# Preparing the bias table of a window-attention kernel: index columns in key-major order, compares ahead of statistics, small transfers of their own

## The reference

```
L0: window attention, windows of 8x8 = 64 tokens, 12 heads of 8 channels, biases on qkv and proj;
    attn = softmax(q k^T / sqrt(8) + rpb_table[rel_index])      rpb_table 225 x 12, rel_index 64 x 64
L1: shifted-window attention, 12 heads of 32 channels; dots + pos_emb[REL] + shift masks
L2: depthwise 3x3 and pointwise 1x1 convolution with ternary weights
L3: spiking attention with batch norms (integer counts 0..4)
```

## Time and profile before

| | |
|---|---|
| device time, 3 runs | 416.7, 419.48, 419.61 us; median 419.48 us |
| the profiled execution's own time | 419.33 us |
| its span, first to last instruction | 416.8 us |
| PE busy | 379.1 us (91%) |
| DVE, ACT, POOL busy | 314.7, 244.1, 200.3 us |
| share of the chain that ended last | PE 59%, DVE 21%, issue 11%, POOL 5%, ACT 2% |

### The profile page before, as it was taken

How to read it: one execution, slowest core, us unless ns; L and a number is a source line. 1 busy time by engine, 2 the same in 40 slices (tenths; PEclk the granted TensorE clock), 3 DMA queues, 4 the chain that set the end, 5 groups by cost and what they waited for, 6 DMA issues and landing times.

```text
span 416.8 us, 13469 instructions
## 1 busy us (share of the span) xinstructions
PE 379.1 (91%) x4953; PEld 275.6 (66%) x4953; DVE 314.7 (75%) x718; ACT 244.1 (59%) x571; POOL 200.3 (48%) x331
## 2 busy tenths in 40 slices
PE   4699999999999999999999999999998999958773
PEld 1588788888878777678777777877776433324441
DVE  3757878777788677978877777778879499856883
ACT  5235566666656555656565566665567355458871
POOL 6564657575767445343444344444444343433331
PEclk9999999999999999999999999999999999988996
DMA  8400000000000000000000000000000000000112
GB/s 187 97 4 4 3 2 0 0 0 0 2 2 3 2 2 2 2 2 2 3 2 0 0 0 0 0 2 0 2 4 2 0 1 0 2 0 19 40 39 57
DMA packets 8343, 5.06 MB, mean 12 GB/s; under 512 B 4874, under 2 KB 8074, under 8 KB 8306
## 3 DMA queue, kind: packets, MB, share of 16 engines
q1 hardware_dynamic: 7456, 4.43, 4.5%
q10 hardware_dynamic: 850, 0.12, 0.2%
HBM read 2.98 MB, written 1.57 MB: 11 GB/s over the span
## 4 chain that ended last, share of the span: by engine, by line
PE 59%; DVE 21%; issue 11%; POOL 5%; ACT 2%; POOLq 0%; DVEq 0%; ACTq 0%
PE bank L860 11%; PE bank L889 10%; PE bank L826 10%; PE bank L869 9%; PE bank L836 6%; DVE conv L1368 6%; PE bank L918 3%; PE bank L933 3%; DVE row_max L1065 3%; POOL y_out L1567 2%; DVE v L1024 2%; DVE stats L681 2%; PE bank L549 2%; PE bank L935 1%; PE bank L1476 1%
## 5 line engine op out<-in xcount | busy, mean ns | idle before, releaser
L1103 POOL TENSOR_TENSOR probs<-probs,row_max 128x384 f32<-128x384 f32 x128 | 105.3, 829 | 118.6 <-DVE row_max L1065 117.7
L967 ACT ACTIVATE probsT<-bank 128x384 f32<-128x384 f32 x128 | 61.1, 492 | 76.2 <-PE bank L869 76.2
L1061 DVE TENSOR_TENSOR probs<-bank,bias 128x384 f32<-128x384 f32 x128 | 65.3, 552 | 52.6 <-PE bank L860 52.3
L1065 DVE TENSOR_REDUCE row_max<-probs 128x6 f32<-128x384 f32 x128 | 68.3, 545 | 1.0
L869 PE MATMUL bank<-cst,probs 128*128 128x128 f32 x384 | 62.9, 281 | 0.0
L889 PE MATMUL bank<-v,probsT 128*64 128x18 f32 (+1 forms) x1536 | 57.7, 219 | 3.5 <-DVE headsN L1090 3.2
L889 PEld LDWEIGHTS bank<-v,probsT 128*64 128x64 f32 x1536 | 50.2, 137 | 15.0 <-issue 13.1
L860 PE MATMUL bank<-k,q 64*64 64x128 f32 x1536 | 58.0, 282 | 1.9 <-ACT k L1012 1.9
L860 PEld LDWEIGHTS bank<-k,q 64*64 64x64 f32 x1536 | 42.3, 135 | 21.8 <-issue 20.8
L1012 ACT ACTIVATE k<-bank,cst 128x256 f32<-128x256 f32 x128 | 54.0, 483 | 0.0
L869 PEld LDWEIGHTS bank<-cst,probs 128*128 128x128 f32 x384 | 44.7, 141 | 11.0 <-issue 5.0
(11 more groups left out here) (142 smaller groups left out, 549.2 us busy)
## 6 DMA issues: line engine op xcount, KB each, us to landing
x<-in_x SPq DMA_DIRECT2D x4, 384.0 KB, 7.3
out_dram<-y_out SPq DMA_DIRECT2D x8, 192.0 KB, 2.1
w<-in_L_conv_w_qkv SPq DMA_DIRECT2D x1, 432.0 KB, 4.9
cst<-in_consts SPq DMA_DIRECT2D x1, 304.0 KB, 5.8
p<-in_L_conv_w_out SPq DMA_DIRECT2D x1, 144.0 KB, 4.6
pos<-in_L_conv_pos_emb SPq DMA_DIRECT2D x8, 2.0 KB
cst<-in_consts SPq DMA_DIRECT2D x1, 117.0 KB, 3.5
w_raw<-in_L_conv_qkv_w ACTq DMA_DIRECT2D x1, 108.0 KB, 5.4
```

What stands on the lines that cost most here:

```text
L967: nc.scalar.activation(probsT[w][:, :], ps_probsT[w % 2][:, 0:NP * 128], ACT.Exp).then_inc(L.s.probsT_sb, 1)
L1061: nc.vector.tensor_tensor(out, scores, b, ALU.add).then_inc(L.s.biased, 1)
L1065: nc.vector.tensor_reduce(row_max[w][:, :], probs[w][:, :, :], AX.X, ALU.max).then_inc(L.s.maxed, 1)
L1103: nc.gpsimd.tensor_tensor(probs[w][:, :, :], probs[w][:, :, :], by_row(row_max[w]), ALU.subtract).then_inc(L.s.shifted, 1)
```

## The change

The diff does seven things. (1) The index copies write `rel_all` with columns in the order (key within a half, key half, query), so that in `onehot` the 128 columns of one key k (both halves, 64 queries each) are adjacent; one matmul with 128 stationary columns serves both halves, and there are 64 in place of 128. The writes of a copy thereby go 128 columns from element to element; a compare takes 64 runs of 16 columns in place of 1024 adjacent ones. (2) All four compares come ahead of the first statistics; the statistics of the third and fourth piece of x come after the bias, and the fourth after the first scores. (3) The identity (8 x 8) and the row numbers (128 x 2) that the spreading and the compares need are transfers of their own, issued by ACT; the bias table and L0's weights are issued by SP, the table behind `cst`, the weights behind the second piece of x. (4) The whole bias comes before the group-norm matmul, v of sample 0 before its scores, and `act_bias` before the evacuation of q. (5) POOL zeroes only `w0T` and `xn` before the table; after it come the rest for L0 and what L1 needs first (`v1`, `w1`), and only then the group norm. ACT's first exponential waits for `w0T` alone. (6) `pe_pos` becomes the extra job of sample 0. (7) The statistics of the second half of the batch are the job of sample 3 in place of sample 1, so samples 2 and 3 are written out and the loop starts at 4.

```diff
         def sp_loads(sp):
             sp.dma_start(cst[:, 0:N_FIRST], a["consts"][:, 0:N_FIRST]).then_inc(const_in, 16)
+            for dst, src in table_loads():
+                sp.dma_start(dst, src).then_inc(table_in, 16)
             n = B // N_X
             for i in range(N_X):
+                if i == N_X // 2:
+                    for dst, src in w0_loads():
+                        sp.dma_start(dst, src).then_inc(w0_in, 16)
                 sp.dma_start(x[:, i * n * T:(i + 1) * n * T].rearrange("c (b t) -> c b t", t=T),
...
+        def small_loads():
+            lo = CONSTS["ident"][0]
+            yield small_ident[:, :], a["consts"][0:REL_ROWS, lo:lo + REL_ROWS]
+            yield rel_of_row[:, :], a["consts"][0:REL_LO, CONSTS["rows"][0]:CONSTS["rows"][1]]
...
         @block.scalar
         def _(act):
-            for dst, src in table_loads():
-                act.dma_start(dst, src).then_inc(table_in, 16)
-            for dst, src in w0_loads():
-                act.dma_start(dst, src).then_inc(w0_in, 16)
+            for dst, src in small_loads():
+                act.dma_start(dst, src).then_inc(small_in, 16)
...
+        zero_first = [w0T[:, :], *(t[C:, :] for t in xn)]
+        zero_next = [p0T[C:, :], *(t[C:, :] for t in heads0), *(t[:, :, :, :] for t in v0)]
+        zero_wide = [*(t[:, :, :, :] for t in v1), w1[C:, :]]
+        zero_late = [w3_parts[C:, :, :], *(t[C:, :] for t in spike_in), spike_a[C:, :], *(t[:, :, :, :] for t in pad)]
...
                 step(nc.gpsimd.tensor_copy(table_parts[0:n_, t, 2, :], table_rest[0:n_, 1, t, :]))
+            for i, t in enumerate(zero_next):
+                nc.gpsimd.memset(t, 0.0).then_inc(zeroed, 1)
+                pool.wait_ge(zeroed, ZEROED_FIRST + i + 1)
+            pool_ones(v0, HD0, zeroed)
+            pool.wait_ge(zeroed, ZEROED)
+            for i, t in enumerate(zero_wide):
+                nc.gpsimd.memset(t, 0.0).then_inc(zeroed_late, 1)
+                pool.wait_ge(zeroed_late, i + 1)
+            pool_ones(v1, HD1, zeroed_late)
+            pool.wait_ge(zeroed_late, ZEROED_WIDE)
             pool.wait_ge(const_in, 16)
             pool_group_norm(pool, 0, 0)
...
+        def by_key(cols):
+
+            return cols.rearrange("r (g q) -> r g q", q=WT)
...
+            dve.wait_ge(small_in, SMALL_IN)
+            step(nc.vector.tensor_copy(small_ident_b[:, :], small_ident[:, :]))
             done["rel_rows"] = count[0]
...
-                cols = slice(2 * i * REL_COLS, 2 * (i + 1) * REL_COLS)
+                of = slice(2 * i * WIN, 2 * (i + 1) * WIN)
                 dve.wait_ge(rel_copied, 2 * i + 2)
                 for t in range(2):
-                    step(nc.vector.tensor_scalar(onehot[:, t, cols], rel_all[:, cols], cst[0:REL_LO, lo + t:lo + t + 1], None,
-                                                 ALU.is_equal))
...
+                    step(nc.vector.tensor_scalar(by_key(onehot[:, t, :])[:, :, of], by_key(rel_all)[:, :, of], rel_of_row[:, t:t + 1],
+                                                 None, ALU.is_equal))
+
+            for i in range(4):
+                compare(i)
+            done["onehot"] = count[0]
+            first_stats(dve, 0)
+            first_stats(dve, 1)
             dve_norm_in(dve, 0, 0)
-            compare(3)
-            done["onehot"] = count[0]
             dve_norm_out(dve, 0, 0)
-            first_stats(2)
-            first_stats(3)
...
         def act_prepare(act):
-            act.wait_ge(zeroed, ZEROED)
+            act.wait_ge(zeroed, ZEROED_W0T)
             nc.scalar.activation(act_first_exp[:, :], w0T[:, 0:1], ACT.Exp).then_inc(first_exp, 1)
+            by_query = rel_all.rearrange("r (k h q) -> r q h k", h=2, q=WT)
             for i in range(REL_ROWS):
                 act.wait_ge(rel_spread, i + 1)
-                nc.scalar.copy(rel_all[:, i * REL_COLS:(i + 1) * REL_COLS], bank[i % 3][:, :]).then_inc(rel_copied, 1)
+                nc.scalar.copy(by_query[:, i * WIN:(i + 1) * WIN],
+                               bank[i % 3][:, :].rearrange("r (q h k) -> r q h k", h=2, k=WT // 2)).then_inc(rel_copied, 1)
...
+                        last = nc.tensor.matmul(bank[2 + i][:, (k - k0_) * 3 * HEADS:(k - k0_ + 1) * 3 * HEADS],
+                                                onehot[0:n, t, k * 128:(k + 1) * 128], table_parts[0:n, t, :, :],
+                                                start=(t == 0), stop=(t == 1))
...
-            one(0)
-            one(1, (0, 1))
-            loop(L0, 2, B - 4)
+            one(0, "pos")
+            one(1)
+            one(2)
+            one(3, (0, 1))
+            loop(L0, 4, B - 4)
...
-            pe_bias(pe, 0, 1)
-            pe_qkv(pe, L0, 0, 0, 2)
-            pe_bias(pe, 1, 3)
+            pe_bias(pe)
+            pe_group_norm(pe, 0, 0)
+            pe_qkv(pe, L0, 0, 0, 3)
             pe_scores(pe, L0, 0, 0)
-            pe_qkv(pe, L0, 0, 2, 3)
             pe_qkv(pe, L0, 1, 0, 2)
-            pe_pos(pe)
...
         def act_first(act):
+            act.wait_ge(zeroed, ZEROED)
             act_norm(act, L0, 0)
+            act_bias(act)
             for i in range(2):
                 evacuate(act, "act", L0, 0, i)
             act_norm(act, L0, 1)
-            act_bias(act)
...
         def dve_first(dve):
             evacuate(dve, "dve", L0, 0, 2)
             dve_scores(dve, L0, 0, 0)
-            dve_pos(dve)
+            first_stats(dve, 3)
+            dve.wait_ge(const_in, 16)
+            prep(nc.vector.tensor_copy(ident_b[:, :], cst[0:C, 0:C]))
```

More of the change, by code:

```diff
@@ L265, in build @@
         rel_in = sem("rel_in")
+        small_in = sem("small_in")
         const_in = sem("const_in")
@@ L380, in late_loads @@
                     yield bn[:, i, j:j + 1], a[f"L3_conv_{name}_{what}"].unsqueeze(1)
-        TABLE_IN, W0_IN, P0_IN, LATE_IN = (16 * len(list(each())) for each in (table_loads, w0_loads, p0_loads, late_loads))
+        SMALL_IN, TABLE_IN, W0_IN, P0_IN, LATE_IN = (
+            16 * len(list(each())) for each in (small_loads, table_loads, w0_loads, p0_loads, late_loads))
         block.sync(sp_loads)
@@ L525, in pe_prepare @@
                 wait(pe, rel_copied, i - 2)
-                nc.tensor.matmul(bank[i % 3][:, :], ident_b[0:REL_ROWS, i:i + 1].broadcast_to([REL_ROWS, 128]), rel_rows_b,
+                nc.tensor.matmul(bank[i % 3][:, :], small_ident_b[:, i:i + 1].broadcast_to([REL_ROWS, 128]), rel_rows_b,
                                  start=True, stop=True).then_inc(rel_spread, 1)
@@ L532, in pe_prepare, with pe_bias @@
             last.then_inc(w0_turned, 1)
-            pe_group_norm(pe, 0, 0)
-        def pe_bias(pe, first, end):
-            if first == 0:
-                pe.wait_ge(rel_copied, REL_ROWS)
-                pe.wait_ge(dve_prep, done["onehot"])
-                pe.wait_ge(table_split, TABLE_STEPS)
-            for i in range(first, end):
+        def pe_bias(pe):
+            pe.wait_ge(rel_copied, REL_ROWS)
+            pe.wait_ge(dve_prep, done["onehot"])
+            pe.wait_ge(table_split, TABLE_STEPS)
+            for i, k0_ in enumerate(range(0, WT // 2, BIAS_KEYS)):
                 if i == 1:
                     pe.wait_ge(w0_copied, NU + 1)
-                k0_ = i * BIAS_KEYS
                 for k in range(k0_, min(k0_ + BIAS_KEYS, WT // 2)):
                     for t, n in ((0, REL_LO), (1, REL - REL_LO)):
-                        for h in range(2):
-                            sel = onehot[0:n, t, :].rearrange("r (q k) -> r q k", k=WT)[:, :, k + h * 32]
-                            last = nc.tensor.matmul(bank[2 + i][h * WT:(h + 1) * WT, (k - k0_) * 3 * HEADS:(k - k0_ + 1) * 3 * HEADS],
-                                                    sel, table_parts[0:n, t, :, :], start=(t == 0), stop=(t == 1))
+                        last = nc.tensor.matmul(bank[2 + i][:, (k - k0_) * 3 * HEADS:(k - k0_ + 1) * 3 * HEADS],
+                                                onehot[0:n, t, k * 128:(k + 1) * 128], table_parts[0:n, t, :, :],
+                                                start=(t == 0), stop=(t == 1))
                 last.then_inc(bias_ready, 1)
@@ L564, in pe_pos @@
                                      start=True, stop=True)
-            nc.tensor.transpose(ps_mix[0:C, 2 * WT:2 * WT + C], p0_raw[:, :], ident[0:C, 0:C]).then_inc(mix_ready, 1)
+            return nc.tensor.transpose(ps_mix[0:C, 2 * WT:2 * WT + C], p0_raw[:, :], ident[0:C, 0:C])
         def dve_pos(dve):
-            dve.wait_ge(mix_ready, 1)
+            dve.wait_ge(weights_ready, 1)
             dve.wait_ge(p0_in, P0_IN)
@@ L578, in pe_weights @@
         def pe_weights(pe, what):
-            if what == "w3":
+            if what == "pos":
+                last = pe_pos(pe)
+            elif what == "w3":
                 pe.wait_ge(late_in, LATE_IN)
@@ L613, in dve_weights_out @@
             step = prep
-            if what == "w3":
-                dve.wait_ge(weights_ready, 1)
+            if what == "pos":
```

(5 more changed lines are left out.)

40 lines of the change are left out of this document (16 added, 24 removed).

## The result

The changed kernel takes 426.47 us (median of 4 runs, 426.2 to 426.68), the kernel before 419.5 (4 runs): 1.020 times the time, 95% interval 1.017 to 1.024. It is slower by 7.0 us, outside the range of 413.5 to 421.2. The profiled execution took 426.2 us, its span 424.4. One execution of before_runs_narrow, 420.9 us, fell in a slower state of the chip and is left out of its figures.

A forecast was written before the change was run, and what follows sets the result against it. PE was taken as the bound, and the unbroken chain before the bodies as what the change shortens: -4.1 for body 0's start, +1.4 position job, +0.6 clock, so -2.1 from 419.33 gives 417.2 us; range 413.5 to 421.2.

The forecast's parts named there:

- Copies in the new order: ACT's eight hopping index copies: 0.50 us each as before, done at 8.5, bounds 8.5 and 12.5.
- Rival (B): Only ACT's index copies get slow, by the upper bound of 4.0 us: 419.5, no change; chance 0.13.
- rival (A): DVE's compares get slow, 1.39 us each, and the sums reach POOL late: 422.9; chance 0.08.
- Weights of L0: Moved to SP's queue: on PE's side there at about 9.0, three transposes 0.8, so the bias starts at 9.9.
- Bias matmuls: PE's 64 wide matmuls at 45 ns, 2.9 us in place of 7.36; bias done at 12.8.
- Rival (C): Wide weight loads on PE are not fast, 100 ns each; bias ends at 16.3: 418.7; chance 0.07.
- Statistics and group norm: DVE's statistics after the compares: group-norm matmul at 13.1, sums ready for POOL at 14.9.
- POOL's list: POOL's table steps and 7.9 us of fills end at 16.6, 1.7 after the sums; 1.4 added to the path.
- To the first scores: From ACT's scaling at 18.6: scores at 22.7, with q, k and v hidden; body 0 at 26.3, 4.1 earlier.
- The position job: Moved from ahead of body 0 into it on PE: 1.1 to 1.7 us, taken as 1.4.
- TensorE's clock: Body 0 starts earlier and may run longer at PE's lower clock level: up to 1.9 us, taken as 0.6.
- Rival (D): PE's clock rises early, for the work from 18.6 on, shortening scores, q, k and body 0: 413.5; chance 0.15.

The follow-up runs named there:

- before_runs_narrow: before_runs with 128 bias matmuls of 64 adjacent stationary columns in place of 64 wide ones: 416.66 us, ratio to the kernel before 0.997.
- copy_runs: The changed kernel with index copies that hop in PSUM and write runs of 8 to the same places: 413.74 us, ratio to the kernel before 0.989.
- runs_narrow: copy_runs with 128 bias matmuls of 64 adjacent stationary columns in place of 64 of 128: 413.61 us.
- cast_order: The changed kernel with the column order made in DVE's cast of the indices, copies in one run, compares in runs of 8: 414.43 us, ratio 0.988.
- runs_pool: copy_runs with POOL's group norm moved ahead of the w1 fill and the small v1 fills: 412.4 us, ratio to the kernel before 0.986.
- before_runs: The kernel before with part (1) alone, its copies writing runs of 8 and hopping in PSUM: 412.71 us, ratio 0.9895.
- flat_copy: The changed kernel with index copies and compares back in one run, wide matmuls kept, bias values in wrong places: 413.93 us, ratio 0.987.
- write_forms: flat_copy with eleven extra ACT and four extra DVE copies of 512 elements in different access forms; 420.8 us, only the copies' durations count.
- query_narrow: flat_copy with 128 bias matmuls of 64 hopping stationary columns, as in the kernel before: 416.2 us, ratio to the kernel before 0.996.
- runs_pos_first: copy_runs with the position job back ahead of sample 0's body: 414.64 us, from 413.17 to 417.01 in six runs.

## Why the prediction was wrong

The step that failed is *Copies in the new order*: "From above one extra pass, 0.5 more each, 4.0 in all", and "I take no extra". It was 1.78 more each, 14.2 in all. The row it leaned on, L494, reads in hops; the copy writes in hops, and the two are not alike: the probes put the source hop at nothing and the single 2-byte write at 1.8 us per 512. Rival (B) had this mechanism, but bounded it by one extra pass. The Trainium skill's rule (Vector Engine (DVE) Microarchitecture Reference, section 5.2 Measured stream behaviour on trn2) pointed the right way. The estimate of 0.34 per copy, worked out from its row for hops of 4 KiB, is a fifth of what ACT paid and under half of the 0.8 of DVE's probe. The same section of the Trainium skill gives 2.50 to 2.51 ns, for 4-byte elements too, when the destination alone steps 24 words every element: as an estimate 0.74 per copy, near the 0.8. When a form occurs in no row, one extra pass is no upper bound.

With the measured size in its place the prediction's own sum holds up to body 0: 14.2 less the slack of 1.7 is 12.5, which put on body 0's 26.3 gives 38.8; it began at 38.62. Between copy_runs and the kernel after lie 12.7 us. The whole time comes out too high, 417.2 + 12.5 = 429.7 against 426.2, by the same 3.5 as without the dear copy, which are accounted for below.

The other steps, by the timeline of copy_runs, the change with that one cost taken away:

- *Start of the spreading*: 4.5 predicted, 4.38 measured. *Compares*: 0.48 predicted, 0.50 to 0.53; rival (A) is out, a compare does not mind runs of 16. *Weights of L0*: bias at 9.9, measured 9.88, but not for the reason given. The transposes were done at 9.64, the last compare at 9.78; in runs_narrow and cast_order too the bias starts 0.10 after the last compare, 0.5 and 0.4 after the transposes. That the number fits is luck.
- *Bias matmuls*: 45 ns, bounds 29 to 100; measured 32.5, 2.08 in all, near the lower bound and below the estimate of 3.4 too. Rival (C) is out: the wide load takes 107 ns but they overlap.
- *Statistics and group norm* and *POOL's list*: sums ready at 14.9, POOL at 16.6; measured about 14.7 (where POOL starts in runs_pool) and 16.36. That POOL's fills decide was right, shown by runs_pool.
- *To the first scores*: 22.7, measured 22.80; body 0 at 26.3, measured 26.30. v does not hide, as the sentence claimed: it waits for the evacuation of q (0.44 at 34.11 in the kernel after) and has the last 1.0 before the scores to itself. The sum came out because two k evacuations and their handovers had been given the same 1.0.
- *The position job* and *TensorE's clock*: 1.4 and 0.6, 2.0 together. Body 1 began at 33.33, 3.9 before the 37.27 of the kernel before: of the 4.1 won only 0.2 went. The job is in body 0, but the higher level of the clock came at its start, not 3.5 us into it as before. Rival (D) had half of that: the scores at 22.80 still took 1.56. The statistics of piece four were not covered, as the prediction had them: on the chain of copy_runs they stand at 26.36, ahead of body 0's adds, and the next scores wait 0.35 for these.
- *A slip in rival (A)*: from 14.9 to 22.3 the sums would be 7.4 later, not 5.4; its 422.9 is right.

So without the dear copy the forecast would have been 3.5 too high (417.2 against 413.74): 1.8 from this last step; 0.7 between body 1 and the end, where the lead grows from 3.9 to the span's 4.6; 0.7 from what lies around the span, 2.5 in the profiled execution of before and 1.8 in that of copy_runs; and 0.3 between that execution, 414.03, and the median.

What stays open is what sets the moment at which the clock rises, and how long it falls again near 370. Among kernels that differ in little, the first PE work at the higher level stands at 22.7 in before_runs (v in 0.88 in place of 1.10), at 26.3 in copy_runs and cast_order (scores in 0.95 and 0.89); in flat_copy the scores at 26.33 still took 1.56 and those at 29.29 took 0.89. The kernel before spreads from 414.9 to 422.0 over all its runs, perhaps for the same reason; only one of its executions has a trace. Why a single 2-byte write costs what it does is not shown either, only where.

## What to carry to other kernels

A layout change has a writing side and a reading side, and they don't cost the same: before a 2-byte result is scattered by single elements, turn the access around so that the source hops and the destination is written in runs; here, with runs of 8, that is worth 12.7 us, and in the probe runs of 2 were already free. A form of access that no row of the trace shows needs a probe or an upper bound far above one extra pass. And test a bundle part by part: here one of seven parts, written well, gives all of the 1.1% that the bundle gives. When two such kernels differ by a few microseconds, look first where the clock rose and fell in each.

## What the runs showed of the hardware

- ACT writing 512 single bf16 elements per partition, 16 or 256 bytes apart, takes 2.4 us against 0.7 in one run; f32, 256 bytes apart, 1.0 against 0.6; DVE, bf16, 256 bytes apart and beside such a copy of ACT, 1.3 against 0.5 (write_forms).
- While ACT writes so, others are slower: POOL's four small fills of `v` took 1.11 and 1.05 us in the kernel after, 0.70 and 0.71 in copy_runs, and 2.50 in write_forms beside ACT's 2.45 and DVE's 1.32. No run takes this apart further.
- Narrow bf16 weight loads (64 columns) follow at 28 ns when their columns lie together and at 56 to 58 when these lie 128 bytes apart; wide ones (128 columns) at 32.5, all at the lower level of the clock (runs_narrow, query_narrow, copy_runs).
- Where TensorE goes to its higher level moves by several us between kernels with nearly the same work (22.7, 26.3, after 33.7), and executions of one kernel, runs_pos_first, lie up to 3.8 us apart, the profiled one with the late rise at the upper end.
- Near 370 us the granted clock falls again for a while: over ten microseconds it was 0.66 of full speed in before_runs_narrow, the kernel before and copy_runs, 0.83 in before_runs.
